# Routing the first two units of the first feed-forward inside the memory stage that precedes it

## The chip, the cores and the metric

The kernel runs on one core of one Trainium2 chip. The metric is the device time of one launch in microseconds. The core's engines are PE (TensorE, matmuls), DVE (VectorE), ACT (ScalarE), POOL (GpSimd) and SP (SyncE, which here issues DMAs and waits). Each runs its own list of instructions in order. They meet only at semaphores: an instruction raises one when it is done, and another engine's list stops at a wait for it.

## What is computed

One block of a hybrid model on `x` of 4 x 1024 tokens, 128 wide (4096 tokens in all), in float32:

```python
x = x + _L0_attn_a_ref(_layernorm(x), ...)   # attention, plus the "memory" term y_ma below
x = x + _L0_ffn_ref(_layernorm(x), ...)      # first feed-forward, in the kernel ffn1
x = x + _L0_attn_b_ref(_layernorm(x), ...)   # a state space scan
x = x + _L0_ffn_ref(_layernorm(x), ...)      # second feed-forward, ffn2

# the second half of attn_a, computed by memory():
e = v[:, :, 1:, :] - y_ar[:, :, :-1, :]
ma = jnp.einsum('bhqd,bhkd->bhqk', qa, ka)           # masked to the lower triangle
y_ma = jnp.einsum('bhqk,bhkd->bhqd', ma, e)
out = merge(y_ar) @ w_proj.T + b_proj + (merge(y_ma) @ w_proj.T + b_proj)

# a feed-forward: a shared part for all tokens, and the best 2 of 8 experts for each
shared = einsum(silu(x @ sw1) * (x @ sw2), sw3)
probs = softmax(x @ rw + rb); w, idx = top_k(probs, 2); w = w / sum(w)
routed = sum over the 2 chosen experts of w * ((silu(x @ ew1[e]) * (x @ ew2[e])) @ ew3[e])
return shared + routed
```

## The kernel before

The launch is a chain of stages, with a barrier of all engines between two of them: `project`, `attention`, `memory`, `ffn` ("ffn1": its parts `route`, then `run_experts`), `scan`, `ffn` again ("ffn2"). Each stage gives its semaphores back at its end.

**memory** (lines 935 to 1244) works through 32 blocks of 128 tokens, `t` = 0 to 31, 8 blocks to a batch. In step `t` of its loop PE computes the raw products of block `t + 1` (L1009, into four PSUM tiles `ps_a`), then the outputs of block `t` (L1032, which needs all masked products of block `t`), adds to the running state (L1058), and in some steps turns the next half batch of `ka` (`turn_ka`, L1048) or projects a finished half (`project_half`, L1067). DVE masks three of the four product tiles (L1084), then the state (L1092), then perhaps adds `x` (L1101) or makes `e` (L1077). ACT copies the fourth product tile out (L1176) and POOL masks it: `mask_last(t)`, L1225. Two waits tie these together: `outputs(t)` on PE waits for DVE's three tiles and for `last_ready`, which `mask_last(t)` raises; `products(t + 2)` wants the PSUM tiles back. The turned `ka` and the projection share one PSUM tile, `ps_p`. Finished halves (512 tokens, 4 blocks) are stored to `x1` in HBM by ACT (`store_x1`, L1161), half `h` in step `4h + 8`, the last two at the end. Once in each batch POOL also widens `e` (L1210, steps with t mod 8 = 5) and adds the bias to `x` (`add_bias`, L1218, t mod 8 = 7).

**route** (L1290 on) takes the tokens in 8 units of 512, the halves of the memory stage. For a unit `u`: DVE takes mean and variance (`mean_dve`), POOL the root (`rstd_of`, L1617, for a group of units at a time), DVE the normalized rows (`norm_dve`, L1370), PE transposes them (`turn_pe`, L1434), ACT copies that out (L1475), PE makes the router's logits (L1441), DVE picks the best two experts (`choose_dve`), PE counts the rows ahead of each (`rank_pe`, L1456, L1458), and DVE works out the row of each token in the table `ex` and labels it (`place_dve`, `label_dve`). Then POOL scatters: 8 indirect DMAs for a unit (L1642), which put normalized rows into `ex` in HBM, grouped by expert. Beside this runs the shared part: `share_pe` (L1449), `silu_act` (L1485), `share_dve` (L1422), `back_pe` (L1467) and `base_dve` (L1428), whose result SP stores to `base`. After the last unit DVE makes a table of tiles (L1678 on) and SP and ACT store padding (L1495).

The order of the work is the order of the code. In `route`, step `s` of PE's loop is: turn unit `s`, `back_pe(s - 2)`, logits of `s`, shared part of `s - 1`, rank of `s`. DVE's step `s` is: place and label unit `s - 1`, normalize `s + 1`, `base_dve(s - 2)`, choose for `s`, shared part of `s - 1`. POOL's list is the root of group 0, four small fills, the root of group 1, an L1629 fill of 128x4160, then the scatters of the units in order, with the roots of groups 2 and 3 after units 0 and 1.

## Time and profile before

| | us |
|---|---|
| median of 3 runs | 1902.08 |
| lowest, highest | 1888.44, 1910.78 |
| the profiled execution, its own time | 1923.11 |
| its span, first to last instruction | 1921.4 |
| mean granted TensorE clock in it | 0.843 of full |

| engine | busy us | share of the span |
|---|---|---|
| PE | 1397.9 | 73% |
| DVE | 1270.6 | 66% |
| ACT | 847.5 | 44% |
| POOL | 879.2 | 46% |

The profile is of one execution; all times of rows are microseconds from the start of its span. The memory stage's steps end at 741 and the routing stage of ffn1 begins at 744.48 (its first DMA) and ends where the experts' first load is issued, at 881.10. Engines are busy in different stages, so the shares above do not say what binds in either.

### The profile page before, as it was taken

The page shows a single profiled execution, that of the slowest core. Times are in us where ns is not written, and L with a number is a line of the kernel's source. Part 1 is how long each engine was busy: PE and PEld are TensorE (multiplying, and loading weights), DVE is VectorE, ACT ScalarE, POOL GpSimd, SP SyncE. Part 2 cuts the span into 40 slices and gives each one's busy share as a digit, 9 for nine tenths or more (in the row PEclk, how much of TensorE's full clock was granted, in tenths as well). Part 3 has the DMA queues.
Part 4 walks back from the last instruction along what each step waited for, and adds up shares of the span by engine and source line. Part 5 has one row for each costly group of instructions (what it writes and reads, how often), then busy time and mean ns, then how long its engine had stood idle before and what let it go on. Part 6 is the DMA issues. An engine that isn't in the chain of part 4 may idle for free. (4 is left out here: it accounts for less than half of the span.)

```text
span 1921.4 us, 27825 instructions
## 1 busy us (share of the span) xinstructions
PE 1397.9 (73%) x8207; PEld 699.9 (36%) x8208; DVE 1270.6 (66%) x2979; ACT 847.5 (44%) x1215; POOL 879.2 (46%) x773
## 2 busy tenths in 40 slices
PE   3459999999999996666884786675875454556883
PEld 1113333333332564445773221221321112435772
DVE  4667999998993566533332388999989995523333
ACT  3404666666667341112442677485573321112441
POOL 3401121121123553652554158879687664652552
PEclk9657999999999897787997797787886666877997
DMA  4721111111121325212223476958859635214225
GB/s 133 232 81 40 49 60 42 56 54 43 61 67 36 87 79 154 65 63 81 78 77 102 141 187 174 235 156 213 200 137 237 153 110 153 64 57 126 76 75 153
DMA packets 218312, 210.68 MB, mean 110 GB/s; under 512 B 49247, under 2 KB 188482, under 8 KB 215874
## 3 DMA queue, kind: packets, MB, share of 16 engines
q1 hardware_dynamic: 196174, 180.70, 35.0%
q0 software_dynamic: 9216, 19.02, 3.0%
q10 hardware_dynamic: 12800, 9.46, 1.6%
q8 instruction: 60, 0.98, 0.2%
q14 instruction: 62, 0.51, 0.1%
HBM read 145.27 MB, written 63.37 MB: 109 GB/s over the span
## 5 line engine op out<-in xcount | busy, mean ns | idle before, releaser
L804 ACT ACTIVATE attn_prob<-attn_ps_cols 128x1024 f32<-128x1024 f32 (+1 forms) x320 | 292.0, 940 | 219.6 <-PE attn_ps_cols L680 218.6
L2386 POOL TENSOR_TENSOR ssm_hc<-ssm_h,ssm_cb 128x1024 f32<-128x1024 f32 x128 | 300.8, 2357 | 137.3 <-DVE ssm_h L2369 113.5
L2369 DVE TENSOR_TENSOR_SCAN ssm_h<-ssm_decay,ssm_ps_u 128x1024 f32<-128x1024 f32 x128 | 292.7, 2287 | 30.9 <-ACT ssm_decay L2357 15.2
L830 POOL TENSOR_SCALAR_AFFINE_SELECT attn_prob<-attn_prob 128x512 f32<-128x512 f32 x128 | 81.2, 634 | 415.9 <-ACT attn_prob L804 415.9
L712 DVE CUSTOM_DVE_ANT_0 attn_ps_rows<-attn_ps_rows,const_mask_rows 128x384 f32<-128x384 f32 (+3 forms) x512 | 236.1, 523 | 39.5 <-PE attn_ps_rows L647 37.4
L647 PE MATMUL attn_ps_rows<-attn_ks,attn_qs 72*128 72x512 bf16 (+3 forms) x768 | 228.9, 352 | 44.2 <-DMA attn_qs<-parts_dram 30.9
L2357 ACT ACTIVATE ssm_decay<-ssm_wide,ssm_aneg 128x1024 f32<-128x1024 f32 x128 | 146.0, 1146 | 173.3 <-DVE ssm_h L2369 97.1
L2320 PE MATMUL ssm_ps_u<-ssm_stack,ssm_spread 96*128 96x512 bf16 x256 | 97.3, 471 | 154.3 <-DVE ssm_h L2369 148.1
L680 PE MATMUL attn_ps_cols<-attn_qs,attn_ks 75*128 75x512 bf16 (+3 forms) x768 | 194.4, 334 | 4.6 <-DMA attn_qs<-attn_nrows 3.9
L699 PE MATMUL attn_ps_o<-attn_prob,attn_vw 128*32 128x512 f32 (+3 forms) x1536 | 166.6, 507 | 0.3 <-POOL attn_prob L830 0.3
L717 DVE TENSOR_REDUCE attn_nm<-attn_ps_rows 128x1 f32<-128x512 f32 x256 | 157.8, 682 | 7.8 <-PE attn_ps_rows L647 7.7
L2364 DVE TENSOR_TENSOR ssm_ps_u<-ssm_ps_u,ssm_bb 128x1024 f32<-128x1024 f32 x128 | 154.8, 1210 | 11.8 <-PE ssm_ps_u L2320 11.8
L647 PEld LDWEIGHTS attn_ps_rows<-attn_ks,attn_qs 72*128 72x128 bf16 x768 | 71.5, 100 | 180.6 <-DVE attn_nm L712 64.9
L1861 POOL DMA_INDIRECT ey_dram<-ffn2e_out,ffn2e_x x80 | 76.8, 960 | 92.3 <-ACT ffn2e_out L1835 70.7
L1861 POOL DMA_INDIRECT ey_dram<-ffn1e_out,ffn1e_x x80 | 76.7, 959 | 86.5 <-ACT ffn1e_out L1835 67.8
L2320 PEld LDWEIGHTS ssm_ps_u<-ssm_stack,ssm_spread 96*128 96x128 bf16 x256 | 17.3, 103 | 252.0 <-DVE ssm_h L2369 203.8
L680 PEld LDWEIGHTS attn_ps_cols<-attn_qs,attn_ks 75*128 75x128 bf16 x768 | 69.9, 100 | 87.8 <-ACT attn_prob L804 35.5
L1810 PE MATMUL ffn1e_ps_h<-ffn1e_xT,ffn1e_w 128*128 128x256 f32 x320 | 81.0, 398 | 18.8 <-ACT ffn1e_xT L1847 16.0
L1810 PE MATMUL ffn2e_ps_h<-ffn2e_xT,ffn2e_w 128*128 128x256 f32 x320 | 79.7, 393 | 19.9 <-ACT ffn2e_xT L1847 19.9
L2336 PE MATMUL ssm_ps_y<-ssm_hc,ssm_gather 128*32 128x512 f32 x512 | 82.9, 779 | 8.6 <-POOL ssm_hc L2386 8.6
L1780 DVE TENSOR_TENSOR ffn2e_hid<-ffn2e_act,ffn2e_ps_h 128x512 f32<-128x512 f32 x40 | 27.5, 688 | 89.6 <-PE ffn2e_ps_h L1810 48.6
L1780 DVE TENSOR_TENSOR ffn1e_hid<-ffn1e_act,ffn1e_ps_h 128x512 f32<-128x512 f32 x40 | 27.5, 688 | 88.0 <-ACT ffn1e_act L1842 71.8
(340 smaller groups left out, 2515.4 us busy)
## 6 DMA issues: line engine op xcount, KB each, us to landing
ssm_wide<-delta_dram SPq DMA_DIRECT2D x128, 512.0 KB, 6.3
attn_ks<-parts_dram SPq DMA_DIRECT2D x48, 192.0 KB
attn_qs<-parts_dram SPq DMA_DIRECT2D x48, 192.0 KB
parts_dram<-proj_parts SPq DMA_DIRECT2D x8, 768.0 KB, 3.8
ffn1e_x<-ex_dram SPq DMA_DIRECT2D x40, 130.0 KB
ffn2e_x<-ex_dram SPq DMA_DIRECT2D x40, 130.0 KB
split_dram<-ssm_parts SPq DMA_DIRECT2D x6, 768.0 KB, 4.4
ssm_stack<-split_dram SPq DMA_DIRECT2D x18, 256.0 KB, 4.6
```

The source lines that it names most:

```text
L647: done = nc.tensor.matmul(out[:, x * w:(x + 1) * w], qs[k][0:KROWS, h, blk * P:(blk + 1) * P], ks[k][0:KROWS, h, half * QW:half * QW + w], ...
L680: done = nc.tensor.matmul(out[:, x, 0:w], ks[k][:, h, j * P:(j + 1) * P], qs[k][:, h, at:at + w], start=True, stop=True, skip_group_check= ...
L699: done = nc.tensor.matmul(ps_o[32 * h:32 * h + 32, at - ch * QW:at - ch * QW + w], vw[k % 2][:, j, h, :], prob[u % RING][:, h, 0:w], start ...
L712: done = nc.vector.tensor_tensor_reduce(scores, scores, c["mask_rows"][:, QW - w:], -1.0, -MINUS, ALU.add, ALU.min, into[:, h, at:at + 1])
L717: nc.vector.tensor_reduce(to, ps_rows[bank][:, 0:len(heads) * w].rearrange("p (h w) -> p h w", w=w), AX.X, ALU.max, negate=True).then_inc( ...
L804: nc.scalar.activation(prob[u % RING][:, heads[0]:heads[-1] + 1, 0:w], ps_cols[s % 2][:].rearrange("p b (x q) -> p (b x) q", x=len(heads) ...
L1810: done = nc.tensor.matmul(ps_h[n][z][:, h, :], w12[z][:, n * HIDDEN + h * P:n * HIDDEN + (h + 1) * P], xT[z][:], start=True, stop=True)
L1861: nc.gpsimd.indirect_dma_start(dram["ey"], bass.IndirectOffsetOnAxis(ap=x[q][:, j, TOKEN:TOKEN + 1].bitcast(I32), axis=0), out[q % OUTS][: ...
L2357: nc.scalar.activation(decay[t % DECAY_RING][:], wide[t % WIDE_RING][:], ACT.Exp, scale=aneg[:, at:at + 1]).then_inc(decay_ready, 1)
L2364: nc.vector.tensor_tensor(ps_u[t % 2][:], ps_u[t % 2][:], bb[b % 2][:], ALU.mult).then_inc(dbx_done, 1)
L2369: nc.vector.tensor_tensor_scan(h[t % H_RING][:], decay[t % DECAY_RING][:], ps_u[t % 2][:], 0.0, ALU.mult, ALU.add).then_inc(scan_done, 1)
L2386: nc.gpsimd.tensor_tensor(hc[:, t % HC_RING, :], h[t % H_RING][:], cb[b % 2][:], ALU.mult).then_inc(hc_done, 1)
```

## The change

Units 0 and 1 of ffn1 are routed (mean to label) in the memory stage, inside its loop, with the 8 scatters of unit 0 in steps 24 to 27. The routing stage then begins with the 8 scatters of unit 1 on POOL, does the shared part of units 0 and 1, and routes units 2 to 7. ffn2 is as before. What was local to `route` becomes a class `Router` that both stages hold; its functions (`mean_dve`, `norm_dve`, `turn_pe` and so on) keep their bodies, except that `choose_dve` is cut in two, the second part now `settle_dve`, and that one scatter has a function of its own. In the memory stage the router's three PSUM outputs all lie in `ps_p`. The groups of roots in ffn1 end at units 1, 2, 3, 5, 7, 8 where they ended at 1, 3, 5, 8.

```diff
+TURNED_BEHIND = {5: 1, 7: 2}
...
-def memory(nc, dram, c, early, a):
+def memory(nc, dram, c, early, a, r):
...
+        r.signals()
+        shared = ps_p[:].rearrange("p h n -> p (h n)")
+        r.ps_x, r.ps_r = shared, shared[:, 0:UPT * EXPERTS].rearrange("p (j e) -> p j e", e=EXPERTS)
+        r.ps_k = shared[:, 0:(UPT + 1) * EXPERTS].rearrange("p (j e) -> p j e", e=EXPERTS)
...
# turn_ka(half), before its other waits
+            if half == 6:
+                nc.tensor.wait_ge(r.xT_ready, 2)
+            if half in TURNED_BEHIND:
+                nc.tensor.wait_ge(r.logits_ready, TURNED_BEHIND[half])
# project_half(half)
+            if half == HALVES - 2:
+                nc.tensor.wait_ge(r.row_ready, AHEAD_UNITS)
+                nc.tensor.wait_ge(r.count_ready, AHEAD_UNITS)
...
# SP
+                    if i == 2:
+                        load_choice(sp, r, a)
+                        for u in range(AHEAD_UNITS):
+                            sp.wait_ge(x1_stored[u], 16)
+                            sp.sem_inc(passed_sp, 1)
+                            sp.dma_start(r.x[u][:], dram["x1"][u * UNIT:(u + 1) * UNIT, :].rearrange("(j p) d -> p j d", p=P)).then_inc(r.x_loaded[u], 16)
# PE, at the end of step t
+                    if t == 15:
+                        pe.wait_ge(x1_ready, 3)
+                        turn_pe(nc, r, c, 0)
+                    if t == 16:
+                        pe.wait_ge(r.r_loaded, 2 * 16)
+                        logits_pe(nc, r, 0)
+                    if t == 19:
+                        pe.wait_ge(r.set_up, 3)
+                        pe.wait_ge(x1_ready, 4)
+                        rank_pe(nc, r, 0)
+                    if t == 20:
+                        pe.wait_ge(r.row_ready, 1)
+                        pe.wait_ge(r.count_ready, 1)
+                        turn_pe(nc, r, c, 1)
+                    if t == 23:
+                        pe.wait_ge(x1_ready, 5)
+                        logits_pe(nc, r, 1)
+                    if t == 27:
+                        pe.wait_ge(x1_ready, 6)
+                        rank_pe(nc, r, 1)
# DVE, at the end of step t
+                    if t == 9:
+                        set_up_dve(nc, r, c, dve)
+                    if t in (12, 15):
+                        mean_dve(nc, r, dve, (t - 12) // 3)
+                    if t in (13, 16):
+                        norm_dve(nc, r, dve, (t - 13) // 3)
+                    if t == 17:
+                        dve.wait_ge(r.r_loaded, 2 * 16)
+                    if t in (17, 24):
+                        choose_dve(nc, r, dve, (t - 17) // 7)
+                    if t in (18, 25):
+                        settle_dve(nc, r, dve, (t - 18) // 7)
+                    if t in (19, 27):
+                        place_dve(nc, r, dve, (t - 19) // 8)
+                    if t in (20, 28):
+                        label_dve(nc, r, dve, (t - 20) // 8)
# ACT, at the end of step t
+                    if t in (14, 17):
+                        twin_act(nc, r, act, (t - 14) // 3)
+                    if t in (15, 20):
+                        turned_act(nc, r, act, (t - 15) // 5)
+                    if t in (19, 26):
+                        tanh_act(nc, r, act, (t - 19) // 7)
# POOL, after mask_last(t)
+                    if t == 2:
+                        set_up_pool(nc, r)
+                    if t in (12, 15):
+                        rstd_pool(nc, r, pool, (t - 12) // 3)
+                    if 24 <= t < 28:
+                        for j in range(2):
+                            scatter(nc, r, dram, pool, 0, (t - 24) * 2 + j)
...
+AHEAD_UNITS, AHEAD_ENDS = 2, [1, 2, 3, 5, 7, UNITS_IN]
...
+def scatter(nc, r, dram, pool, u, j):
+
+    k = u % DEEP
+    if j == 0:
+        pool.wait_ge(r.xn_ready, u * UPT + UPT)
+        pool.wait_ge(r.twin_ready, u + 1)
+        pool.wait_ge(r.id_ready, u + 1)
+        pool.wait_ge(r.gate_ready, u + 1)
+        pool.wait_ge(r.pos_ready, u + 1)
+        pool.sem_inc(r.passed, 1)
+    n, j = j // UPT, j % UPT
+    nc.gpsimd.indirect_dma_start(dram["ex"], bass.IndirectOffsetOnAxis(ap=r.pos[k][:, n, j:j + 1], axis=0),
+                                 r.xn[k][:, n, j, :], None).then_inc(r.sent[k], 16)
...
+def rstd_pool(nc, r, pool, g):
+
+    at = r.group_of(r.ends[g] - 1)
+    pool.wait_ge(r.veps_ready, g + 1)
+    pool.sem_inc(r.passed, 1)
+    nc.gpsimd.tensor_tensor(r.rstd[:, at], r.veps[:, at], r.power[:, at], ALU.pow).then_inc(r.rstd_ready, 1)
...
# route(), first = 2 in ffn1 and 0 in ffn2; PE
-                pe.wait_ge(s_loaded, 5 * 16)
...
+                pe.wait_ge(s_loaded, 3 * 16)
+                pe.wait_ge(r.r_loaded, 2 * 16)
+                pe.wait_ge(r.ready, 5)
+                pe.wait_ge(r.set_up, 3)
+                for u in range(first - 1):
+                    share_pe(u, 0)
+                    share_pe(u, 1)
+                for s in range(first, UNITS_IN + 2):
...
# DVE, ahead of its loop from s = first
+                for u in range(first - 1):
+                    share_dve(dve, u, 0)
+                    share_dve(dve, u, 1)
+                dve.wait_ge(r.r_loaded, 2 * 16)
+                dve.wait_ge(r.set_up, 3)
+                choose_dve(nc, r, dve, first)
+                settle_dve(nc, r, dve, first)
+                norm_dve(nc, r, dve, first + 1)
# POOL
+                if first:
+                    for j in range(0, 3):
+                        scatter(nc, r, dram, pool, held, j)
+                rstd_pool(nc, r, pool, group)
...
```

POOL's list in the memory stage, from step 5 to step 16 (L1225 before and L1285 after are `mask_last`, one for each block; `mem_ew` is the widening, `mem_xb` the bias). Before:

```order
L1210 COPY mem_ew<-mem_e 128x32x8 x4
L1225 TENSOR_TENSOR mem_am<-mem_raw,const_strict 128x512 x2
L1218 TENSOR_TENSOR mem_xb<-mem_x_in,mem_bias 128x1024
L1225 TENSOR_TENSOR mem_am<-mem_raw,const_strict 128x512 x6
L1210 COPY mem_ew<-mem_e 128x32x8 x4
L1225 TENSOR_TENSOR mem_am<-mem_raw,const_strict 128x512 x2
L1218 TENSOR_TENSOR mem_xb<-early_x,mem_bias 128x1024
L1225 TENSOR_TENSOR mem_am<-mem_raw,const_strict 128x512 x6
```

After, in the same place:

```order
L1285 TENSOR_TENSOR mem_am<-mem_raw,const_strict 128x512 x5
L1559 TENSOR_TENSOR ahead_rstd<-ahead_veps,ahead_power 128x4
L1285 TENSOR_TENSOR mem_am<-mem_raw,const_strict 128x512
L1270 COPY mem_ew<-mem_e 128x32x8 x4
L1285 TENSOR_TENSOR mem_am<-mem_raw,const_strict 128x512 x2
L1278 TENSOR_TENSOR mem_xb<-early_x,mem_bias 128x1024
L1559 TENSOR_TENSOR ahead_rstd<-ahead_veps,ahead_power 128x4
L1285 TENSOR_TENSOR mem_am<-mem_raw,const_strict 128x512 x6
```

The roots of units 0 and 1 now stand between the masks of blocks 12 and 13, and of 15 and 16.

PE's list at the opening of ffn1's routing stage (`ps_x` transposes, `ps_r` logits, `ps_k` rank, `ps_h` shared part, `ps_o` its way back). Before:

```order
L1434 MATMUL ffn1r_ps_x<-const_ident,ffn1r_xn 128x128 x4
L1441 MATMUL ffn1r_ps_r<-ffn1r_rw,ffn1r_xnT 128x8 x4
L1456 MATMUL ffn1r_ps_k<-ffn1r_chosen,ffn1r_before 128x40
L1458 MATMUL ffn1r_ps_k<-ffn1r_chosen,ffn1r_ones 128x32
L1458 MATMUL ffn1r_ps_k<-ffn1r_chosen,ffn1r_ones 128x24
L1458 MATMUL ffn1r_ps_k<-ffn1r_chosen,ffn1r_ones 128x16
```

After:

```order
L1623 MATMUL ffn1r_ps_h<-ahead_xnT,ffn1r_sw 128x512 x4
L1495 MATMUL ffn1r_ps_x<-const_ident,ffn1r_xn 128x128 x4
L1630 MATMUL ffn1r_ps_o<-ffn1r_sw,ffn1r_hid 128x128 x8
L1503 MATMUL ffn1r_ps_r<-ahead_rw,ahead_xnT 128x8 x4
L1623 MATMUL ffn1r_ps_h<-ahead_xnT,ffn1r_sw 128x512 x4
L1512 MATMUL ffn1r_ps_k<-ahead_chosen,ahead_before 128x40
```

The shared part of unit 0 stands ahead of the transpose of the first unit to be routed there, and `back_pe(0)` and the shared part of unit 1 stand between that transpose and the rank.

POOL's list from the opening of that stage on (L1550 is a scatter, x32 are the 8 each of units 4 to 7). After:

```order
L1550 DMA ex_dram<-ahead_xn,ahead_pos 36864x130 x3
L1559 TENSOR_TENSOR ahead_rstd<-ahead_veps,ahead_power 128x8
L1781 MEMSET ffn1r_zeros 128x4160
L1783 IOTA ffn1r_zeros 128x32
L1550 DMA ex_dram<-ahead_xn,ahead_pos 36864x130 x2
L1550 DMA ex_dram<-ffn1r_xn,ffn1r_pos 36864x130 x8
L1559 TENSOR_TENSOR ahead_rstd<-ahead_veps,ahead_power 128x8
L1550 DMA ex_dram<-ffn1r_xn,ffn1r_pos 36864x130 x8
L1559 TENSOR_TENSOR ahead_rstd<-ahead_veps,ahead_power 128x4
L1550 DMA ex_dram<-ffn1r_xn,ffn1r_pos 36864x130 x32
```

Before, the list held x8, a root, x8, a root and x48 in their place; the stage now has 56 scatters where it had 64.

## Rows read from the trace of the kernel before

**Rows 1.** Stages: us; PE, PEld, DVE, ACT, POOL busy (instructions), granted clock, DMA.

```profile
622.00:744.00 122.00, 114.77 (x1540) 74.24 (x1538) 76.59 (x134) 44.00 (x75) 59.46 (x55) 0.93 0.28 80
744.00:764.00 20.00, 5.31 (x26) 4.37 (x26) 14.01 (x72) 2.90 (x5) 8.98 (x14) 0.50 0.91 265
764.00:867.00 103.00, 68.28 (x293) 44.67 (x293) 47.69 (x279) 17.75 (x37) 65.21 (x66) 0.78 0.27 76
```

**Rows 2.** Timeline of the routing stage: start, us, engine, line, [idle before <-releaser].

```profile
744.48 0.37 SPq L1501 DMA_DIRECT2D ffn1r_x<-x_dram  x1
763.49 1.23 POOL L1642 DMA_INDIRECT ex_dram<-ffn1r_xn,ffn1r_pos  x1 [3.64 <-DVE ffn1r_xn L1370]
...
817.28 0.96 POOL L1642 DMA_INDIRECT ex_dram<-ffn1r_xn,ffn1r_pos  x1 [8.56 <-DVE ffn1r_xn L1370]
...
845.92 0.96 POOL L1642 DMA_INDIRECT ex_dram<-ffn1r_xn,ffn1r_pos  x1 [8.73 <-DVE ffn1r_xn L1416]
...
865.89 0.96 POOL L1642 DMA_INDIRECT ex_dram<-ffn1r_xn,ffn1r_pos  x1 [0.31 <-issue]
881.10 0.43 SPq L1756 DMA_DIRECT2D ffn1e_x<-ex_dram  x1
```

**Rows 3.** Timeline of DVE in the routing stage, same columns.

```profile
811.32 0.69 DVE L1428 TENSOR_TENSOR ffn1r_base<-ffn1r_ps_o,ffn1r_x 128x512 f32<-128x512 f32 x1 [12.44 <-remote]
```

**Rows 4.** Timeline of ffn2's routing stage: its last scatter, the next stage's first load.

```profile
1725.81 0.96 POOL L1642 DMA_INDIRECT ex_dram<-ffn2r_xn,ffn2r_pos  x1 [0.30 <-issue]
1746.41 8.45 SPq L1756 DMA_DIRECT2D ffn2e_x<-ex_dram  x8
```

**Rows 5.** Timeline of the memory stage, POOL's masks of blocks 12, 13, 16.

```profile
670.52 1.28 POOL L1225 TENSOR_TENSOR mem_am<-mem_raw,const_strict 128x512 f32<-128x512 f32 x1 [2.76 <-ACT mem_raw L1176]
673.67 1.28 POOL L1225 TENSOR_TENSOR mem_am<-mem_raw,const_strict 128x512 f32<-128x512 f32 x1 [1.86 <-ACT mem_raw L1176]
...
684.71 1.26 POOL L1225 TENSOR_TENSOR mem_am<-mem_raw,const_strict 128x512 f32<-128x512 f32 x1
```

**Rows 6.** Timeline of the memory stage, DVE and PE in steps 12 to 16.

```profile
674.84 0.29 DVE L1092 TENSOR_TENSOR mem_state<-mem_ps_s,const_same_head 128x128 f32<-128x128 f32 x1
676.67 1.08 PE L1032 MATMUL mem_ps_y<-mem_am,mem_ew 128*32 128x128 f32 x32
...
683.79 1.89 DVE L1084 TENSOR_TENSOR mem_am<-mem_ps_a,const_strict 128x512 f32<-128x512 f32 x3 [0.43 <-PE mem_ps_a L1009]
687.21 1.08 PE L1032 MATMUL mem_ps_y<-mem_am,mem_ew 128*32 128x128 f32 x32
```

**Rows 7.** Timeline of routing, its opening: DVE's first mean, POOL's root.

```profile
747.35 0.87 DVE L1353 BATCH_NORM_STATS2 ffn1r_stats<-ffn1r_x 128x6 f32<-128x128 f32 x4 [1.83 <-DMA ffn1r_x<-x_dram]
749.01 1.04 POOL L1617 TENSOR_TENSOR ffn1r_rstd<-ffn1r_veps,ffn1r_power 128x4 f32<-128x4 f32 x1 [3.90 <-DVE ffn1r_veps L1360]
```

**Rows 8.** Timeline of routing, PE at either clock.

```profile
751.68 1.09 PE L1434 MATMUL ffn1r_ps_x<-const_ident,ffn1r_xn 128*128 128x128 f32 x4 [10.73 <-DVE ffn1r_xn L1370]
764.79 6.30 PE L1449 MATMUL ffn1r_ps_h<-ffn1r_xnT,ffn1r_sw 128*128 128x512 f32 x8
773.82 0.96 PE L1441 MATMUL ffn1r_ps_r<-ffn1r_rw,ffn1r_xnT 128*128 128x8 f32 x8
796.76 2.05 PE L1467 MATMUL ffn1r_ps_o<-ffn1r_sw,ffn1r_hid 128*128 128x128 f32 x16 [0.23 <-DVE ffn1r_hid L1422]
799.46 3.68 PE L1449 MATMUL ffn1r_ps_h<-ffn1r_xnT,ffn1r_sw 128*128 128x512 f32 x8
```

**Rows 9.** Timeline of routing, DVE and POOL about the fill.

```profile
756.81 2.81 DVE L1387 CAST ffn1r_order<-ffn1r_index 128x32 f32<-128x32 uint32 x1
756.02 3.56 POOL L1629 MEMSET ffn1r_zeros<- 128x4160 f32 x1
```

**Rows 10.** Timeline of the memory stage's first steps, POOL.

```profile
634.32 1.27 POOL L1225 TENSOR_TENSOR mem_am<-mem_raw,const_strict 128x512 f32<-128x512 f32 x1 [1.63 <-ACT mem_raw L1176]
639.56 1.27 POOL L1225 TENSOR_TENSOR mem_am<-mem_raw,const_strict 128x512 f32<-128x512 f32 x1 [3.96 <-ACT mem_raw L1176]
```

More of the change, by code:

```diff
@@ L1272, in past, with ffn @@
     return not isinstance(s, int) or s >= n
[L1275 removed]
+def ffn(nc, dram, c, a, stage, src, dst, router=None):
     with ExitStack() as ctx:
@@ new lines, in norm_dve, with choose_dve @@
+def norm_dve(nc, r, dve, u):
+    k = u % DEEP
+    dve.wait_ge(r.rstd_ready, sum(end <= u for end in r.ends) + 1)
+    if u >= DEEP:
+        dve.wait_ge(r.sent[k], u // DEEP * (TOP * UPT * 16))
+        dve.wait_ge(r.xT_made, u - DEEP + 1)
+    for j in range(UPT):
+        at = u * UPT + j
+        nc.vector.tensor_scalar(r.xn[k][:, 0, j, 0:D], r.x[k][:, j, :], r.mv[:, at, 0:1], r.rstd[:, at:at + 1],
+                                ALU.subtract, ALU.mult).then_inc(r.xn_ready, 1)
+def choose_dve(nc, r, dve, u):
+    dve.wait_ge(r.r_done, u + 1)
+    nc.vector.tensor_tensor(r.logits[:], r.ps_r[:], r.rb[:].unsqueeze(1).broadcast_to([P, UPT, EXPERTS]), ALU.add).then_inc(r.logits_ready, 1)
+    dve.wait_ge(r.logits_ready, u + 1)
+    for j in range(UPT):
+        nc.vector.max(r.top[:, j, :], r.logits[:, j, :]).then_inc(r.top_ready, 1)
+    dve.wait_ge(r.top_ready, u * UPT + UPT)
+    for j in range(UPT):
+        nc.vector.max_index(r.index[:, j, :], r.top[:, j, :], r.logits[:, j, :]).then_inc(r.index_ready, 1)
@@ new lines, in label_dve, with turn_pe @@
+def label_dve(nc, r, dve, u):
+    k = u % DEEP
+    nc.vector.tensor_copy(r.xn[k][:, :, :, TOKEN].bitcast(I32), r.ids[:, :, u * UPT:(u + 1) * UPT]).then_inc(r.id_ready, 1)
+    dve.wait_ge(r.tanh_ready, u + 1)
+    nc.vector.tensor_scalar(r.xn[k][:, :, :, GATE], r.tanh[:], 0.5, 0.5, ALU.mult, ALU.add).then_inc(r.gate_ready, 1)
+def turn_pe(nc, r, c, u):
+    nc.tensor.wait_ge(r.xn_ready, u * UPT + UPT)
+    nc.tensor.wait_ge(r.xT_ready, u)
+    for j in range(UPT):
+        done = nc.tensor.transpose(r.ps_x[:, j * P:(j + 1) * P], r.xn[u % DEEP][:, 0, j, 0:D], c["ident"][:])
+    done.then_inc(r.xT_made, 1)
@@ L1326, in route @@
-        x_loaded, stored = [m.sem(f"x_ld{k}") for k in range(DEEP)], m.pair("stored")
-        stat, mean, veps_ready, rstd_ready, xn_ready, xT_made = (m.sem(n) for n in ("stat", "mean", "veps", "rstd", "xn", "xT_made"))
-        xT_ready, r_done, logits_ready, top_ready, index_ready, order_ready = (m.sem(n) for n in ("xT", "r_done", "logits", "top", "index", "order"))
-        gap_ready, tanh_ready, gate_ready, pick_ready, chosen_ready = (m.sem(n) for n in ("gap", "tanh", "gate", "pick", "chosen"))
@@ L1330, in route @@
[L1330 to L1334 removed]
+        s_loaded, counted, stored = m.sem("s_ld"), m.sem("counted"), m.pair("stored")
@@ L1585, in _ @@
+                    if s == first + 2:
+                        for u in range(first + 5, UNITS_IN):
+                            mean_dve(nc, r, dve, u)
                     if 1 <= s <= UNITS_IN:
```

431 lines of the change are left out of this document (209 added, 222 removed).

## The prediction

> **What bounds the kernel now.** I read the stages first, then the timeline of each engine about the two places that the change touches, then the waits. In the memory stage PE is busy for 114.8 of 122 us, at 0.93 of full clock, and every other engine has room [rows 1]. So a microsecond put on PE there, or a wait of PE there, is a microsecond of the launch. In the routing stage of ffn1 nothing is busy throughout: PE 68, DVE 48 and POOL 65 of 103 us. There the thing to see is POOL's row of scatters. The first starts at 763.49, 19.0 us after the stage's first DMA at 744.48, the last ends at 866.85, and the experts' first load goes out at 881.10: 19.0 + 103.4 + 14.3, in all 136.6 us [rows 2]. A unit's 8 scatters take 8 x 1.26 = 10.1 us, which is 81 us for eight units, some 5 us go to roots between them, and two idle gaps of 8.56 and 8.73 us make up most of the rest. These gaps are strange and matter here. DVE sat 12.44 us until 811.32 before an add that waits for PE alone in effect, and the release is not put down to an engine [rows 3]; POOL's previous run of scatters had ended at 817.28 - 8.56 = 808.72. I read it as: when 16 scatters run back to back, DVE and ACT learn of PE's work only some 2.6 us after the last of them, and the next unit then needs about 6 us more. I call this the hold. What causes it I can't tell from the profile. It occurred behind units 2 and 3 and again behind 4 and 5, not behind 0 and 1, where a root stands between the two.
>
> **What the change takes from the routing stage.** Its first unit is now unit 2, and six units follow instead of eight.
>
> The opening gets longer. PE must first do the shared part of unit 0. The shared weights' load stands behind two small loads less, some 1.0 us of SP's queue (my estimate from the 0.37 to 0.43 us that an issue takes on SP [rows 2], two of them and the gaps), so PE starts at 751.68 - 744.48 - 1.0 = 6.2 us into the stage [rows 8], where before the transposes went. Shared part at half clock, 6.30: 12.5. The transpose of unit 2 hides in the wait for silu and product of unit 0 (1.6 us, estimated from two elementwise operations of 0.6 and 0.7 us and their hand-overs): 14.1. `back_pe(0)` 2.05: 16.2. Logits 0.96: 17.1. Shared part of unit 1 at full clock, 3.68: 20.8. Silu and product again 1.6: 22.4. Placing and labelling 1.2, and 1.2 to POOL's first scatter: 24.8 us, against 19.0 before. I take half clock for the first and full clock for the rest, since PE is busy without a break here: in the rows the same shared part takes 6.30 us at 764.79 and 3.68 at 799.46 [rows 8]. All at half clock would add 2.05 + 0.96 + 2.6 = 5.6 us. POOL's 8 scatters of unit 1 (10.1 us) and the fill of 3.56 us lie inside these 24.8 us, of which POOL has 12 to 13 us of other work at most, so they cost nothing; without that cover they would cost what passes 24.8.
>
> From the first scatter on, the six units repeat what units 0 to 5 did, since code and order are the same: from 763.49 to 845.92 - 8.73 = 837.19, 73.7 us [rows 2]. One root is of 4 columns and not 12, 1.3 us less (1.04 for 4 columns [rows 7]; 2.3 for 12 is an estimate by columns). The last scatter so ends at 24.8 + 72.4 = 97.2 us, where it ended at 122.4.
>
> The tail behind the last scatter was 14.3 us here, but 1746.41 - 1726.77 = 19.6 in ffn2 [rows 2, 4], whose last pair of units ran without the short gap that ffn1's had. In the forecast the last pair is like the pair of units 4 and 5, without a gap, so I take 19.6. The stage becomes 116.8 us where it was 136.6: **19.8 us less**. The bounds: 25 us less with the short tail, 14 with everything in the opening at half clock.
>
> **What it puts on the memory stage.** PE: a transpose of 4 (0.55, half of the 1.09 at half clock), logits (0.96), rank (0.2), for two units: 3.4 us on the engine that bounds the stage [rows 8].
>
> Then the waits. In step 12 POOL's list has the root of unit 0 behind `mask_last(12)`, and the root waits for DVE's mean, which DVE begins only when it has masked block 13 and the state, at 675.1 [rows 6]. From the mean's start to the root's start takes 1.66 us and the root 1.04 [rows 7]: 677.8. Only then comes `mask_last(13)`, 1.28 us: 679.1, where it ended at 674.95 before [rows 5]. PE wanted it at 676.67 [rows 6]: **2.4 us** of standstill. In step 15 the same: block 16 is masked on DVE until 685.7, root done at 688.4, `mask_last(16)` done at 689.7 instead of 685.97, PE wants it at 687.21, less the transpose that PE has now in between (0.5): **2.0 us**. Behind PE's wait stand the state and the next products, and DVE, ACT and POOL all wait for those; nothing hides it. `turn_ka(5)` now waits for DVE to take the logits of unit 0, behind the mask of the state (0.29) and an add: 0.7 us. DVE's inserts of 0.9 to 1.4 us use idle time of about 0.8 in each step; I put 0.8 us for all. POOL in steps 24 to 27 has 1.28 + 2 x 1.26 = 3.8 us of work in steps of 3.15 us (670.52 to 673.67 [rows 5]) to 4 us; PE takes a mask up to 1.7 us after it is ready (674.95 to 676.67), which covers most of the 2 to 3 us of delay: 0.5 us. ACT's six small copies fit. The loads from `x1` are issued and land some 6 us ahead of need (a load took 747.35 - 744.48 = 2.9 us [rows 2, 7]). Sum: 3.4 + 2.4 + 2.0 + 0.7 + 0.8 + 0.5 = **9.8 us more**. Low bound 5 (the root waits half hidden), high bound 15 (DVE's inserts and the scatters wholly on the path).
>
> One cost no row of the memory stage can show, that DVE and POOL get in each other's way. In routing the cast of 128x32 took 2.81 us and ended just as POOL's fill of 3.56 us did [rows 9]. In the memory stage DVE's inserts lie behind its own masks, at a time when POOL's mask of the same block is over, so I cost it at nothing. The Trainium skill (SBUF — State Buffer, Who interferes with whom) says that DVE copies, casts and scalar operations in their two-port modes, and operations with two SBUF inputs beside a reading GpSimd operation, wait until GpSimd's whole operation is over. The row agrees for the fill. By that rule the sum would be larger wherever an insert meets a mask or POOL is late; that is a rival below.
>
> **Sum.** 9.8 - 19.8 = -10.0 us. Against the profiled execution 1923.1 gives 1913. The median of the runs shown is 21 us lower than that execution; I carry the difference over: 1902.1 - 10.0 = **1892 us**. This way alone holds 1883 to 1900.
>
> **The rivals.**
> The forecast: 0.52.
> The hold goes. With the shorter last root, unit 4's start moves against PE's work, and if unit 6 is ready before the hold sets in, the gap of 8.7 us is gone, and the tail may be the short one (5.3 us). Against it: all four such pairs of the two routing stages with followers had their gap. -10 - 8.7 - 5.3 = -24: 1878. 0.17.
> The hold costs more. Opening at half clock (5.6 us), and one more gap of 8.6 since the scatters start later: +4: 1906. The clock in the first 20 us was 0.50 [rows 1]. 0.15.
> POOL and DVE collide. Five inserts for each unit (norm, choose, settle, place, label) could each wait out one POOL operation of 1.28 us: up to 12.8 us, +2.8: 1905. It decides where POOL runs late, behind the roots and in steps 24 to 27. 0.06.
> **Slower than before:** PE's clock falls in the memory stage. There PE has one standstill after another in steps 13 to 28 where it had none. After its 11 us of idleness before 751.68 it stood at 0.50 [rows 1, 8]. A block at half clock took 639.56 - 634.32 = 5.2 us instead of 3.15 [rows 10, 5]: 2.1 us each. From five blocks on the gain is gone; over twelve, 25 us, the launch takes 1917. Against it: standstills of 2.4 us are much shorter than that idleness. The Trainium skill (TensorE: Matmul & The Clock Gate, What's actually happening) says that the default is throttled and that activity releases it; the trace agrees, at 0.50 before and 0.93 in a busy stage. 0.07.
> The change doesn't do what it says: unit 1's load or label is late and PE waits for it in the memory stage, which eats all of it: 1902. 0.03.
>
> **Range and chances.** From the hold gone to the opening at half clock, with the bounds of the memory stage: 1876 to 1907. A measurement of this kernel tells about 1% from no change, 19 us; its runs spread over 22. Faster than 1883: most of the second case and the low end of the first, 0.26. Slower than 1921: 0.05. Within: 0.69.
>
> **What would show it.** The routing stage takes 117 us, its first scatter of unit 2 25 us in, one gap of 8 to 9 us before unit 6, 19.6 us behind the last. In the memory stage two waits of PE of 2 to 2.5 us before the outputs of blocks 13 and 16, and 10 us more in all. I am wrong if the gap is missing, if PE's clock in the memory stage is under 0.9, or if the first scatter of unit 2 is past 30 us.

## The result, and the profile after

The changed kernel takes 1896.17 us (median of 19 runs, 1879.20 to 1910.04), the kernel before 1905.38 (19 runs, 1888.44 to 1922.76). The ratio is 0.9939, 95% interval 0.9918 to 0.9960: 11.6 us less by the ratio, 9.2 by the medians, where 10 were forecast. The forecast was 1892 us and its range 1876 to 1907. The gain is under the 1% that the prediction called no change, though the interval leaves 1 out. The profiled execution took 1897.15 us, its span 1895.4.

In the two profiles the routing stage goes from 744.48 to 881.10 before and from 754.86 to 863.85 after: 136.6 and 109.0 us. The memory stage, from the last mask of block 12 (670.52 before, 668.27 after) to the stage's end, takes 74.0 and 86.6. So +12.6 and -27.6; the forecast had +9.8 and -19.8. The two spans differ by 26.0; the 11 us beyond -15.0 lie partly ahead of block 12 (2.3) and mostly (8.7) in later stages whose code did not change. I take them for scatter between executions; the profiled execution of the kernel before, 1923.11 us, is longer than any of its 19 runs.

First the stages of the profile after, columns as in [rows 1]:

```profile
622.00:754.00 132.00, 119.34 (x1575) 78.17 (x1574) 88.27 (x218) 46.75 (x81) 69.86 (x70) 0.95 0.28 81
754.00:777.00 23.00, 14.61 (x64) 8.79 (x65) 12.94 (x68) 5.48 (x9) 15.87 (x16) 0.78 0.99 284
777.00:853.00 76.00, 50.51 (x232) 33.78 (x230) 38.52 (x211) 12.83 (x26) 49.07 (x50) 0.82 0.25 74
```

The memory stage as a whole keeps its clock, 0.95 (0.93 before); the rival in which it falls for good did not come.

The memory stage after, timeline, about steps 12 and 15:

```profile
674.45 1.04 POOL L1559 TENSOR_TENSOR ahead_rstd<-ahead_veps,ahead_power 128x4 f32<-128x4 f32 x1 [4.90 <-DVE ahead_veps L1425]
675.46 1.26 POOL L1285 TENSOR_TENSOR mem_am<-mem_raw,const_strict 128x512 f32<-128x512 f32 x1
676.87 1.93 PE L1037 MATMUL mem_ps_y<-mem_am,mem_ew 128*32 128x128 f32 x32 [2.39 <-POOL mem_am L1285]
...
688.95 1.03 POOL L1559 TENSOR_TENSOR ahead_rstd<-ahead_veps,ahead_power 128x4 f32<-128x4 f32 x1 [2.51 <-DVE ahead_veps L1425]
689.95 2.50 POOL L1285 TENSOR_TENSOR mem_am<-mem_raw,const_strict 128x512 f32<-128x512 f32 x2
691.36 1.08 PE L1037 MATMUL mem_ps_y<-mem_am,mem_ew 128*32 128x128 f32 x32 [2.23 <-POOL mem_am L1285]
```

POOL stands 4.90 us at the root, the mask behind it is late, and PE stands 2.39 and 2.23 us, against 2.4 and 2.0 forecast. What was not forecast is the first row of PE: the outputs took 1.93 us instead of 1.08. The windows of PE alone (its busy time, count and granted clock in each stretch) show why: full clock ahead of the standstill, 1.2 GHz behind it. Behind the second standstill the outputs still run at full clock, and the fall comes 2 us later, in the products.

```profile
672.00:674.40 2.40, 2.40 (x21) 1.00 0.21 57
676.80:679.00 2.20, 2.13 (x33) 0.50 0.00 0
693.50:697.00 3.50, 3.50 (x22) 0.53 1.16 349
```

```profile
693.58 1.99 PE L1014 MATMUL mem_ps_a<-early_qm,early_kaT 32*128 32x512 f32 x8
```

The routing stage after, timeline; it answers to [rows 2]:

```profile
754.86 0.37 SPq L1647 DMA_DIRECT2D ffn1r_x<-x_dram  x1
760.99 5.88 PE L1623 MATMUL ffn1r_ps_h<-ahead_xnT,ffn1r_sw 128*128 128x512 f32 x8 [9.66 <-DMA ffn1r_sw<-in_L_ffn_sw_dram]
777.74 0.96 POOL L1550 DMA_INDIRECT ex_dram<-ffn1r_xn,ffn1r_pos  x1 [3.99 <-DVE ffn1r_xn L1436]
814.52 0.96 POOL L1550 DMA_INDIRECT ex_dram<-ffn1r_xn,ffn1r_pos  x1 [3.97 <-DVE ffn1r_xn L1436]
843.00 0.95 POOL L1550 DMA_INDIRECT ex_dram<-ffn1r_xn,ffn1r_pos  x1 [8.60 <-DVE ffn1r_xn L1488]
851.97 0.96 POOL L1550 DMA_INDIRECT ex_dram<-ffn1r_xn,ffn1r_pos  x1 [0.30 <-issue]
863.85 0.43 SPq L1904 DMA_DIRECT2D ffn1e_x<-ex_dram  x1
```

Unit 2's first scatter comes 22.9 us in, six units last 75.2, and 10.9 us follow the last scatter. One gap of 8.60 stands where [rows 2] had two; it stands before unit 7, not unit 6. Its cause, PE and its two listeners while units 5 and 6 are scattered (814.5 to 834.4):

```profile
820.72 0.64 PE L1495 MATMUL ffn1r_ps_x<-const_ident,ffn1r_xn 128*128 128x128 f32 x4
825.77 0.60 ACT L1524 ACTIVATE ahead_xnT<-ffn1r_ps_x 128x512 f32<-128x512 f32 x1 [4.62 <-remote]
821.59 2.05 PE L1630 MATMUL ffn1r_ps_o<-ffn1r_sw,ffn1r_hid 128*128 128x128 f32 x16 [0.23 <-DVE ffn1r_hid L1610]
837.04 0.69 DVE L1616 TENSOR_TENSOR ffn1r_base<-ffn1r_ps_o,ffn1r_x 128x512 f32<-128x512 f32 x1 [14.33 <-remote]
```

PE's transposes end at 821.36 and ACT, idle, starts on them at 825.77. `back_pe` ends at 823.64 and DVE, idle, starts at 837.04, 13.4 us later.

### The profile page after: what moved, and what is told of

It reads as the page before. It is cut to its first block and busy times, and to the rows that moved or that the text cites. A ratio compares the mean times of both kernels' runs of the same rounds, so it can differ in the third digit from the quotient of the medians.

```text
span 1895.4 us, 27842 instructions
## 1 busy us (share of the span) xinstructions
PE 1386.3 (73%) x8207; PEld 690.9 (36%) x8208; DVE 1268.0 (67%) x2981; ACT 845.2 (45%) x1215; POOL 881.2 (46%) x775
## 5 line engine op out<-in xcount | busy, mean ns | idle before, releaser
L680 PEld LDWEIGHTS attn_ps_cols<-attn_qs,attn_ks 75*128 75x128 bf16 x768 | 69.8, 100 | 87.6 <-ACT attn_prob L804 35.5
```

The lines of the kernel that those rows point to most:

```text
L680: done = nc.tensor.matmul(out[:, x, 0:w], ks[k][:, h, j * P:(j + 1) * P], qs[k][:, h, at:at + w], start=True, stop=True, skip_group_check= ...
```

## The experiments

They ran in four groups, each on a chip of its own, beside runs of the kernel before. That kernel took 1803 and 1804 us in the first and the last group (E1 to E4, E12) and 1910 and 1911 in the others (E5 to E8, E9 to E11), and 1905 in the runs of the result. Theory A and theory B are the two that each expectation names. "The hold" is the prediction's word for DVE and ACT learning late of PE's finished work while POOL scatters. Compare ratios within a group, and stages with this in mind. Of each the memory stretch (mask of block 12 to mask of block 31: 65.1 in the kernel before, 77.7 in the changed), the routing stage of ffn1, and the ratio:

| | before takes | memory | routing | ratio (95%) |
|---|---|---|---|---|
| E1 roots later | 1803 | 69.8 | 89.8 | 0.9906 (0.9881 to 0.9931) |
| E2 changed, spacer | 1803 | 77.7 | 88.8 | 0.9972 (0.9953 to 0.9991) |
| E3 before, spacer | 1803 | 65.1 | 106.5 | 1.0003 (0.9988 to 1.0019) |
| E4 one unit | 1803 | 71.8 | 98.1 | 0.9991 (0.9975 to 1.0008) |
| E5 changed again | 1910 | 76.2 | 109.9 | 0.9939 (0.9902 to 0.9975) |
| E6 scatters in opening | 1910 | 77.5 | 121.6 | 0.9986 (0.9953 to 1.0020) |
| E7 weights early | 1910 | 69.9 | 108.9 | 0.9881 (0.9846 to 0.9916) |
| E8 spacer again | 1910 | 77.9 | 109.2 | one run, 1904.28 us |
| E9 product first | 1911 | 69.9 | 109.8 | 0.9877 (0.9835 to 0.9919) |
| E10 paced | 1911 | 77.7 | 105.6 | one run, 1882.03 us |
| E11 scatters last | 1911 | 76.2 | 127.1 | one run, 1933.30 us |
| E12 all, paced | 1804 | 69.9 | 104.1 | 1.0128 (1.0108 to 1.0148) |

**E1.** The two roots one step later.

```diff
-                    if t in (12, 15):
-                        rstd_pool(nc, r, pool, (t - 12) // 3)
+                    if t in (13, 16):
+                        rstd_pool(nc, r, pool, (t - 13) // 3)
```

> The changed kernel, with the two roots of the memory stage one step later in POOL's list (behind the masks of blocks 13 and 16 instead of ahead of them). Theory A (the two standstills of PE, 2.39 and 2.23 us, and the stretches at half clock behind them are the price of the roots' place): PE no longer waits for POOL before the outputs of blocks 13 and 16, the clock holds, and the stretch from mask_last(12) to the routing stage's first load, 86.6 us in the changed kernel, shortens by 5 to 9 us; the launch by as much, ratio to the kernel before about 0.990. Theory B (the half clock there has another cause, or the wait moves to DVE, whose norm of unit 0 now waits for the later root): the stretch shortens by less than 3 us, and either the half clock stays or new waits on DVE stand in steps 14 and 17.

The stretch is 7.9 us shorter than that of the changed kernel (77.7): A. In E1's timeline the roots wait 0.40 and 1.28 us instead of 4.90 and 2.51, and the outputs run at 1.08:

```profile
675.98 1.08 PE L1037 MATMUL mem_ps_y<-mem_am,mem_ew 128*32 128x128 f32 x32
676.04 1.04 POOL L1559 TENSOR_TENSOR ahead_rstd<-ahead_veps,ahead_power 128x4 f32<-128x4 f32 x1 [0.40 <-DVE ahead_veps L1425]
677.05 1.27 POOL L1285 TENSOR_TENSOR mem_am<-mem_raw,const_strict 128x512 f32<-128x512 f32 x1
```

Two standstills of 4.6 us together cost 7.9. Nearly all of the other 3.3 is the half clock behind them: in the profile after, outputs, state and `turn_ka` of step 13 take 1.5 us more than the same rows of E1 (1.93, 0.80 and 0.97 against 1.08, 0.49 and 0.60), and the products and outputs behind the second standstill 1.6 more. (E1's ratio is 11.9 us under E2's, its median 8.4; E2 carries the spacers.) A surprise stands in the same trace: 32 scatters in a row, 794.7 to 835.0, and no gap.

**E2, E3.** A memset of 8 columns on POOL between units without a root, in both kernels (E3 has `rstd_of(u + 2)` under `if u < 2`).

```diff
+        spacer = m.sb("spacer", [P, UNITS_IN, EXPERTS])
...
                     if group + 2 + u - first < len(r.ends):
                         rstd_pool(nc, r, pool, group + 2 + u - first)
+                    else:
+                        nc.gpsimd.memset(spacer[:, u], 0.0)
```

> The changed kernel, with one small memset (8 columns) on POOL between the scatters of units where no root stands, in both routing stages with followers. Theory A (the hold comes of more than 8 scatters in a row, and an operation of POOL's engine between them breaks it): the gap of 8.6 us before unit 7's scatters in ffn1 and both gaps in ffn2 shrink to under 4 us; about 6 us less in ffn1's routing stage and 12 in ffn2's, the launch some 15 us less, ratio to the kernel before about 0.985. Theory B (the root breaks it by its wait for DVE, or by its length, or the hold is the scatters' own load on memory and independent of what stands between): the gaps stay at 8 to 9 us and the time is that of the changed kernel, 0.994.

> The kernel before, with the same small memset on POOL between the scatters of units where no root stands. Theory A (it breaks the hold): the two gaps of 8.56 and 8.73 us in ffn1 and the two in ffn2 shrink under 4 us, some 20 us less in all, ratio 0.989. Theory B (it does not): ratio 1.000, gaps as they were. If A holds here and in the changed kernel, the change's gain without the hold is the distance between the two.

The gaps were gone, but they were gone in E1 too, which has no spacer. So these two don't test it. They show something else: without the hold the kernel before has a routing stage of 106.5 us, not 136.6, and the change (88.8) takes 17.7 us from it and puts 12.6 on the memory stage. That is -5.1; the ratio says 5.0 (0.9972 against the kernel before) or 5.6 (against E3). The changed kernel without spacers was not run on this chip.

**E4.** One unit ahead; unit 1's work and unit 0's scatters taken out of the memory stage.

```diff
-AHEAD_UNITS, AHEAD_ENDS = 2, [1, 2, 3, 5, 7, UNITS_IN]
+AHEAD_UNITS, AHEAD_ENDS = 1, [1, 2, 4, 6, UNITS_IN]
...
-                    if t == 20:
...
-                        rank_pe(nc, r, 1)
...
-                    if 24 <= t < 28:
-                        for j in range(2):
-                            scatter(nc, r, dram, pool, 0, (t - 24) * 2 + j)
```

> The changed kernel with one unit routed ahead instead of two: unit 0 in the memory stage as before, its scatters in the opening of the routing stage, unit 1 and the rest in the routing stage. Seven units' scatters follow, with roots behind units 1 and 2. Theory A (each unit ahead takes 10.1 us of scatters out of the routing stage, and the opening pays for the shared part): memory stage +5 to +6 against the kernel before (one standstill of 2.4 and its half clock), routing stage 136.6 - 10 + 1 + or - a hold; with units 3 and 4, 5 and 6 in pairs and 7 alone, two gaps of 8.6 and a short tail of 11: about 120 us. Together -11 to -13 us: as good as two units or a little better. Theory B (the gain comes of the number of gaps and the short tail alone, not of the moved scatters): the routing stage is within 3 us of that of the changed kernel, 109.

A's sum missed, since it had two gaps in it and there was none. But each unit does take its scatters' time out: 106.5, 98.1, 88.8 for none, one and two. It puts 6.7 and then 5.9 on the memory stage. B fell. (E4 has no spacers, E2 and E3 have.)

**E5.** The changed kernel, unaltered.

> The changed kernel once more, beside the next three, since the kernel before took 1803 us in the last experiments and 1905 us where the change was first timed, and the gaps of 8.6 us behind 16 scatters were missing there. Theory A (the hold belongs to the chip that a run falls on, and part of the change's gain is the one gap that it saved): where the kernel before takes about 1803 us the routing stage of the changed kernel takes 88 to 90 us without a gap and the ratio is 0.996 to 0.998; where it takes about 1905 us the gaps are back and the ratio is 0.994. Theory B (the gain does not depend on the hold): ratio 0.994 in either case.

The ratio is 0.9939 again, and the routing stage takes 109.9 us with a gap of 8.6. In this case both theories gave 0.994, so the ratio does not choose between them; that the gap is back is A's. What speaks for A is E2's ratio beside this one, and the two intervals overlap.

The memory stretch, 76.2, tells more of the clock. Both standstills are there (2.40 and 2.23 us), and behind the first the outputs take 1.82; behind the second the clock holds:

```profile
685.30 1.08 PE L1037 MATMUL mem_ps_y<-mem_am,mem_ew 128*32 128x128 f32 x32 [2.23 <-POOL mem_am L1285]
687.52 1.14 PE L1014 MATMUL mem_ps_a<-early_qm,early_kaT 32*128 32x512 f32 x8
```

The same products took 1.99 in the first profile, and that is the 1.5 us between 76.2 and 77.7. Of seven profiles with both standstills five show the second fall (memory 77.5 to 77.9) and two, E5 and E11, do not (76.2).

**E6.** Unit 0's eight scatters go from steps 24 to 27 (taken out as in E4) to the head of POOL's list in the routing stage.

```diff
+                for j in range(TOP * UPT if first else 0):
+                    scatter(nc, r, dram, pool, 0, j)
                 if first:
                     for j in range(0, 3):
                         scatter(nc, r, dram, pool, held, j)
```

> The changed kernel with the 8 scatters of unit 0 taken out of steps 24 to 27 of the memory stage and put first in POOL's list of the routing stage. Theory A (they cost the memory stage next to nothing, 0.5 us, and POOL's room in the opening, some 5 us beside 18 of work, does not hold their 10.1): the memory stage 0.5 to 1.5 us shorter, unit 2's first scatter 5 to 7 us later in the routing stage, the launch 4 to 6 us longer than the changed kernel. Theory B (in the memory stage the scatters delay masks that PE waits for, by up to 4 us): memory 4 us shorter, launch within 2 us of the changed kernel.

A, but dearer: memory 77.5, with both falls of the clock (77.7 to 77.9 in the profiles of the changed kernel that have both, so 0.2 to 0.4 less), unit 2's first scatter 35.6 us in instead of 22.0 (E5), the ratio 0.0047 (9 us) above E5's. In the memory stage the eight cost about nothing, in the routing stage 12.

**E7.** E1, with `sw1`, `sw3` in the `Router` and their three loads behind `load_choice` in the memory stage.

```diff
+                        load_shared(sp, r, a)
...
-        sw1, sw3 = m.sb("sw1", [P, 2, HIDDEN]), m.sb("sw3", [P, HC, D])
+        sw1, sw3 = r.sw1, r.sw3
```

> The changed kernel with the roots one step later, and with the shared expert's three weight matrices loaded in the memory stage, so that PE need not wait for them in the opening of the routing stage. Theory A (the opening is bounded by PE's chain, which begins with that load): unit 2's first scatter comes 3 to 4 us earlier in the stage, at 19 to 20 us instead of 23, where POOL's own work (some 19 us) takes over; the launch 3 to 4 us under that of the roots alone, ratio 0.988 to 0.989. Theory B (POOL's own work or the shared part at half clock bounds it): under 1 us.

PE starts the shared part at 746.33, 0.4 us into the stage (6.1 before), and yet unit 2's first scatter comes at 23.1. The timeline of E7:

```profile
753.17 0.66 PE L1504 MATMUL ffn1r_ps_x<-const_ident,ffn1r_xn 128*128 128x128 f32 x4 [1.05 <-DVE ffn1r_xn L1445]
757.18 3.58 PE L1639 MATMUL ffn1r_ps_o<-ahead_sw,ffn1r_hid 128*128 128x128 f32 x16 [3.35 <-DVE ffn1r_hid L1619]
755.84 1.28 DVE L1619 TENSOR_TENSOR ffn1r_hid<-ffn1r_act,ffn1r_ps_h 128x512 f32<-128x512 f32 x2
```

PE now waits for a product that DVE does only at 755.84, behind means whose `x` has to be loaded. A falls; B's number came (no earlier scatter) but not its cause: the list of DVE bounds it. The launch is still 0.0058 below E5, 11 us, of which 6.3 is the memory stretch and the rest within the two intervals.

**E8.** E2's kernel, on a chip where the kernel before takes 1910 us.

> The kernel with the small memset between the units' scatters once more, for one look, in case this is a chip on which the hold shows. Theory A (an operation of POOL's engine between the units breaks the hold): PE's semaphore updates reach DVE and ACT within 0.1 us, and no gap stands before unit 7's scatters. Theory B (the memset does not matter): the gap of 8.6 us is there as in the changed kernel, and updates come up to 13 us late. On a chip without the hold both give no gap, and it tells nothing.

Theory A falls. E8's timeline:

```profile
833.85 0.13 POOL L1794 MEMSET ffn1r_spacer<- 128x8 f32 x1
835.16 0.69 DVE L1617 TENSOR_TENSOR ffn1r_base<-ffn1r_ps_o,ffn1r_x 128x512 f32<-128x512 f32 x1 [12.68 <-remote]
842.29 0.97 POOL L1550 DMA_INDIRECT ex_dram<-ffn1r_xn,ffn1r_pos  x1 [8.31 <-issue]
```

**E9.** E7, with `share_dve` of unit 0 ahead of the means of units 3 and 4.

```diff
                     if u == first:
                         norm_dve(nc, r, dve, u)
-                for u in range(first - 1):
-                    share_dve(dve, u, 0)
-                    share_dve(dve, u, 1)
+                        for v in range(first - 1):
+                            share_dve(dve, v, 0)
+                            share_dve(dve, v, 1)
```

> The kernel with later roots and early shared weights, and in DVE's list of the opening the product of unit 0's shared part set ahead of the means of units 3 and 4. Theory A (with the weights there in time, PE waited 3.35 us for that product, which stood behind 2.5 us of means; the product's place is now what bounds the opening): unit 2's first scatter comes 2.5 to 3.5 us earlier, at 19.5 to 20.5 us into the stage instead of 23.1, where POOL's own 19 us take over; the launch 3 us less, ratio to the kernel before 0.986 to 0.987 where that takes 1905 us, and 0.988 or so where it takes 1803. Theory B (the clock of PE, at half in this opening, bounds it): under 1 us, ratio as in the last experiment, 0.988.

`back_pe` starts at 747.91, 8.6 us into the stage (11.3 in E7), but the first scatter comes at 22.2: 0.9 us won, not 3. That is B's number, but not B's cause, since `back_pe` took 2.05 us, at full clock. The timeline of E9 shows who took the rest:

```profile
752.48 3.55 POOL L1789 MEMSET ffn1r_zeros<- 128x4160 f32 x1
752.51 3.56 DVE L1466 CAST ahead_order<-ahead_index 128x32 f32<-128x32 uint32 x1
761.60 0.96 POOL L1559 DMA_INDIRECT ex_dram<-ffn1r_xn,ffn1r_pos  x1 [2.85 <-DVE ffn1r_xn L1445]
```

A cast that takes 0.17 to 0.41 us away from the fill in E5 and E7 took 3.56 and ended with POOL's fill, as in [rows 9]. The Trainium skill (SBUF — State Buffer, Who interferes with whom) says that a DVE cast in a two-port mode is blocked for the whole of GpSimd's instruction when that one was issued first; both rows agree, the fill starting 0.03 us ahead here and 0.79 there.

**E10.** A longer pause, behind every second scatter.

```diff
+        spacer, paced = m.sb("spacer", [P, 1160]), m.sem("paced")
...
+                        if j % 2 and j < TOP * UPT - 1:
+                            pool.wait_ge(paced, paces)
+                            nc.gpsimd.memset(spacer[:], 0.0).then_inc(paced, 1)
+                            paces += 1
...
```

> The changed kernel with a memset of about 1 us on POOL behind every second scatter of the routing stages. For a chip on which PE's updates come late. Theory A (they are late because the scatters come one upon another, and a pause lets them through): in the routing stages no update of PE is over 1.5 us late; 6 units of 10.1 + 3 us, 79 us, follow the first scatter without a gap, against 75 now with gaps of 3.9 and 8.6. Theory B (the presence of scatters is enough, whatever their spacing, as in the experts' stage, where they come one by one): updates stay late by several us and the stage grows by the pauses, 18 us, less what the gaps hide of them. On a chip without late updates both give 79 us and nothing is told apart.

A. The waits of DVE while the six units are scattered, in total, times and longest; E5 first, then E10, then E1 of the other group:

```profile
DVE ffn1r_base L1616 <- remote: 20.1, 2, 15.0
DVE ffn1r_base L1616 <- PE ffn1r_ps_o L1630: 3.9, 2, 2.5
```

```profile
DVE ffn1r_base L1617 <- PE ffn1r_ps_o L1631: 2.0, 3, 0.9
```

```profile
DVE ffn1r_base L1616 <- PE ffn1r_ps_o L1630: 3.5, 3, 1.7
```

With the pauses the wait whose releaser the trace can't name is gone, as it is where the kernel before takes 1803 us. Each of the 32 times that DVE or ACT takes up PE's transposes, logits, ranks or `back_pe` in this stage, it starts within 0.14 us of PE's end or of its own last work; in E9, on the same chip, it is up to 10.5 us late. In E10's timeline `back_pe` ends at 818.15 between two scatters and DVE starts at 818.19:

```profile
816.10 2.05 PE L1631 MATMUL ffn1r_ps_o<-ffn1r_sw,ffn1r_hid 128*128 128x128 f32 x16 [0.23 <-issue]
816.15 1.08 POOL L1794 MEMSET ffn1r_spacer<- 128x1160 f32 x1
818.19 0.69 DVE L1617 TENSOR_TENSOR ffn1r_base<-ffn1r_ps_o,ffn1r_x 128x512 f32<-128x512 f32 x1 [0.90 <-PE ffn1r_ps_o L1631]
```

Six units take 80.4 us without a gap, the tail 2.6. The stage's 105.6 us stand against 108.9 to 109.9 in the five profiles with the hold and the scatters in the same place (the first, E5, E7, E8, E9); ffn2's routing stage takes 129 us where E5's took 142. The launch time, 1882.03, shows no gain by itself: it is one run, 17 us under E5's median but inside E5's spread (1881.33 to 1904.21).

**E11.** All scatters of units 2 to 7 behind the last unit's places.

```diff
+                for g in range(group + 2, len(r.ends)):
+                    rstd_pool(nc, r, pool, g)
+                pool.wait_ge(r.pos_ready, UNITS_IN)
                 for u in range(first, UNITS_IN):
                     for j in range(TOP * UPT):
                         scatter(nc, r, dram, pool, u, j)
```

> The changed kernel with all scatters of units 2 to 7 issued behind the last unit's places, instead of each behind its own unit. Theory A (scatters under way are what makes PE's updates late): with no scatter under way while PE works through units 3 to 7 every one of PE's updates comes within 0.1 us of its matmul's end, a unit takes PE and DVE 7 to 8 us, and unit 7's places are ready some 40 us behind unit 2's; then 48 scatters of 1.26 us in a row, 60 us. The stage about 23 + 40 + 60 + 4 = 127 us instead of 109. Theory B (PE's updates are late in the routing stage for another cause, its own clock or DVE's work): late updates of over 1 us stand in the part without scatters too, and the gaps with them. If this chip shows no late updates at all, only the durations are told.

A in its first half, and 127.1 us as reckoned. E11's timeline on both sides of the first scatter:

```profile
797.23 2.05 PE L1630 MATMUL ffn1r_ps_o<-ffn1r_sw,ffn1r_hid 128*128 128x128 f32 x16 [0.23 <-DVE ffn1r_hid L1610]
799.32 0.69 DVE L1616 TENSOR_TENSOR ffn1r_base<-ffn1r_ps_o,ffn1r_x 128x512 f32<-128x512 f32 x1 [1.03 <-PE ffn1r_ps_o L1630]
806.21 1.04 POOL L1550 DMA_INDIRECT ex_dram<-ffn1r_xn,ffn1r_pos  x1 [23.51 <-DVE ffn1r_pos L1480]
810.77 2.05 PE L1630 MATMUL ffn1r_ps_o<-ffn1r_sw,ffn1r_hid 128*128 128x128 f32 x16 [0.84 <-DVE ffn1r_hid L1610]
817.10 0.40 DVE L1847 CAST ffn_firsti<-ffn_first 1x40 int32<-1x40 f32 x1
817.53 0.69 DVE L1616 TENSOR_TENSOR ffn1r_base<-ffn1r_ps_o,ffn1r_x 128x512 f32<-128x512 f32 x1
```

From 766 to 806 us no scatter is issued, and DVE starts 0.04 us behind PE's end at 799.28. The last add, at 817.53, comes 4.7 us behind PE's end at 812.82, with scatters under way, but it shows no hold: it has no idle time before it, since DVE was making the table of tiles until 817.50. So this trace shows that without scatters there is no hold; that it comes with them rests on the first profile and on E5, E8 and E9, where PE and DVE do the same work beside them.

**E12.** The edits of E9 and E10 together.

> The changed kernel with all that helped: roots one step later, shared weights loaded in the memory stage, the product of unit 0 ahead of the means, and the memset of 1.1 us behind every second scatter of the routing stages. Theory A (the parts add up, and the pauses pay where PE's updates come late): memory stage 8 us shorter than the changed kernel's; the routing stages about 105 and 129 us or, with the earlier start of unit 2, 103; the launch 0.978 to 0.983 of the kernel before where that takes 1905 us. On a chip without late updates the pauses only cost: 6 and 8 units at 3 us each, some 35 us less what the shorter tails give back, ratio 0.997 to 1.004. Theory B (the pauses gave no gain and the one run that showed 1882 us was a low one): 0.987 to 0.990 where the kernel before takes 1905.

It ran where the kernel before takes 1804 us, and there the pauses only cost: routing 104.1 in ffn1 against E1's 89.8, 129.2 in ffn2 against 106.5. The 14.3 and 22.7 make 37 us on top of E1's 1790, and the median is 1825.82. The ratio expected, 0.997 to 1.004, had too much in it for shorter tails: ffn1's is 2.6 us, and E1's was 3.4. What it does where the hold shows was not measured. Of the versions timed more than once there, E9 (0.9877) and E7 (0.9881) are the best and not told apart, and their intervals just overlap E5's. On the other chips E1 is the best (0.9906), clear of E2's interval.

## Why the prediction was right, and where it was not

**The mechanism held.** Six units instead of eight, one gap instead of two, a longer opening, two waits for a root.

**Opening**, 24.8 forecast, 22.9 measured. PE started at 6.1 (6.2) and the shared part took 5.88 (6.30); `back_pe` came 0.83 us behind it, not 1.6. The hand-overs were counted too dear.

**Six units**, 72.4 forecast, 75.2 measured: a gap of 3.97 before unit 5 that the kernel before did not have there. So my rule for the hold, 16 in a row, was too narrow: within runs of 8 too DVE took up `back_pe`'s result 3.2 us late (799.10 to 802.32), and ACT, free from 810.63 on, took up transposes that had ended at 807.88 only at 812.40.

**Tail**, the failed term: 19.6 forecast, 10.9 measured, 8.7 us. I took the last two units for a pair, as in ffn2. There DVE stood idle until 2.7 us behind the last scatter, and the last unit's shared part came after that (timeline of the kernel before):

```profile
1729.50 0.69 DVE L1428 TENSOR_TENSOR ffn2r_base<-ffn2r_ps_o,ffn2r_x 128x512 f32<-128x512 f32 x1 [13.25 <-remote]
```

Here the pair was units 5 and 6. Unit 7 came alone behind the gap, with the work of PE and DVE done up to it, and `back_pe` of unit 7 ended at 850.73, ahead of the last scatter's end at 852.93.

**Memory stage**, 9.8 forecast, 12.6 measured. The standstills were sized right (4.6 against 4.4) but E1 prices them at 7.9, with the half clock behind them (6.3 between E5, where the clock fell once, and E7): the rival of the clock, for two blocks instead of twelve. What remains, 4.7, answers to the 5.4 of PE's work, DVE's inserts, `turn_ka` and the scatters; E6 agrees that the scatters cost next to nothing.

The terms sum to -15.0 in one pair of profiles; the many runs say -11.6. That the forecast of -10.0 came so near was in part luck: the tail was off by 8.7 us, and the memory stage and the six units by 2.8 each the other way. And the number seems to hold only where the hold shows: where it does not, E2, with spacers, gives -5.0 (0.9953 to 0.9991, against 0.9918 to 0.9960).

**The hold.** I had "16 in a row" as its condition and a root as what breaks it. The runs put this in its place. It needs scatters under way (E11), it goes with pauses of 1.1 us behind every second one (E10), a pause of 0.13 us between units does nothing (E8), and it does not come everywhere: in E1 32 scatters in a row passed without it. E8, E10 and E11 are one profile each. Whether the length of the pauses or their number matters was not tried. Two more places speak for the run of scatters: in the memory stage, where they come in twos, the stretch is as long with the hold as without it (77.7 in the first profile and in E2; 69.9 in E7 and 69.8 in E1), and in the experts' stage, where they come mostly in fours in the slower traces, it is some 24 us longer. Why PE's signals are late is open. That it is the chip, and not its condition at the time, is inferred from the groups alone; each chip was seen once.
